# Far edges between the 40th and 41st chunk, biases as rows, index tables worked off later: one change to a graph network and attention kernel

## The reference

```python
aggr = segment_sum(edge_features, receivers_idx, num_segments=num_vertex)
collected = concatenate([layernorm(x), aggr], axis=-1)
h = relu(collected @ W1 + b1)
h = relu(h @ W2 + b2)
x = x + h @ W3 + b3
# then slice attention on layernorm(x): softmax((xn @ W_x + b_x) @ W_slice + b_slice) / temp),
# tokens, attention over 64 slices in 8 heads, and the projection back, added to x
```

## Time and profile before

| | us |
|---|---|
| median of 3 runs | 737.33 |
| the profiled execution's own time | 737.38 |
| its span, first to last instruction | 735.60 |
| first stage: last `first_layer_x` of the stream ends | 286.91 |
| second stage: first `layer1` matmul (L1187) starts | 292.46 |
| PE busy / DVE busy over the span | 711.6 / 408.2 |

### The profile page before, as it was taken

The page is one execution under the profiler, slowest core; times in us unless marked ns, Lnnn a source line. Parts: engine busy times, 40 slices in busy tenths (PEclk is TensorE's granted clock), DMA queues, the critical chain, the costliest instruction groups (busy, mean ns, idle before and its releaser), DMA issues.

```text
span 735.6 us, 12565 instructions
## 1 busy us (share of the span) xinstructions
PE 711.6 (97%) x3716; PEld 456.6 (62%) x3716; DVE 408.2 (55%) x989; ACT 245.5 (33%) x462; POOL 237.3 (32%) x306
## 2 busy tenths in 40 slices
PE   6999999999999997999999989999999999899997
PEld 3666666666666665665666645555555554588886
DVE  6654554554554565244443587878787878522222
ACT  4234333333333344222212133333333333223331
POOL 3101101101110104033233255555656565144441
PEclk8999999999999999999999999999999999999999
DMA  8999999999999995100000000000000000012222
GB/s 318 384 378 415 405 410 410 405 405 407 404 405 406 383 382 173 29 0 0 0 0 0 0 2 0 0 0 0 0 0 0 0 0 1 0 53 76 71 79 70
DMA packets 43233, 118.99 MB, mean 162 GB/s; under 512 B 4937, under 2 KB 19229, under 8 KB 38095
## 3 DMA queue, kind: packets, MB, share of 16 engines
q1 hardware_dynamic: 42399, 118.50, 42.0%
q10 hardware_dynamic: 816, 0.26, 0.2%
HBM read 112.35 MB, written 6.40 MB: 161 GB/s over the span
## 4 chain that ended last, share of the span: by engine, by line
PE 77%; DMA 19%; DVE 2%; issue 1%; SPq 1%; ACT 0%; POOL 0%; DVEq 0%; ACTq 0%; POOLq 0%
DMA ring_mem<-edge_attr_in 18%; PE ps L1089 14%; PE ps L1336 12%; PE ps L1252 11%; PE ps L1260 11%; PE ps L1187 6%; PE ps L1205 6%; PE ps L1195 6%; PE ps L1269 3%; PE ps L1142 3%; PE ps L1244 1%; PE ps L1102 1%; PE ps L1134 1%; DVE big L800 0%; PE ps L1044 0%
## 5 line engine op out<-in xcount | busy, mean ns | idle before, releaser
L1089 PE MATMUL ps<-ring_mem,side 128*64 128x256 f32 x1564 | 188.0, 387 | 7.1 <-DMA ring_mem<-edge_attr_in 5.0
L1089 PEld LDWEIGHTS ps<-ring_mem,side 128*64 128x64 f32 x1564 | 112.6, 138 | 68.2 <-issue 27.5
L717 DVE TENSOR_TENSOR side<-iota_w,rel 128x512 f32<-128x512 f32 x98 | 67.1, 686 | 93.0 <-PE ps L1102 92.8
L1260 PE MATMUL ps<-side,ring_mem 128*128 128x512 f32 x196 | 92.3, 593 | 1.0 <-ACT ring_mem L655 1.0
L1252 PE MATMUL ps<-ring_mem,xn 128*128 128x512 f32 x196 | 92.3, 593 | 0.6 <-DVE ring_mem L952 0.6
L619 ACT ACTIVATE side<-ps 128x256 f32<-128x256 f32 (+1 forms) x98 | 40.6, 414 | 144.4 <-PE ps L1089 142.8
L512 POOL TENSOR_TENSOR var_e<-mv,eps 128x2 f32<-128x2 f32 (+1 forms) x25 | 4.9, 194 | 236.4 <-DVE mv L783 236.4
L800 DVE TENSOR_TENSOR big<-big,ps 128x128 f32 x223 | 63.9, 286 | 30.8 <-issue 12.3
L1336 PE MATMUL ps<-side,ring_mem 128*128 128x256 f32 x360 | 77.9, 379 | 0.0
L566 POOL TENSOR_TENSOR ring_mem<-ring_mem 128x512 f32<-128x512 f32 x49 | 66.9, 1366 | 30.9 <-DVE ring_mem L952 30.9
L1336 PEld LDWEIGHTS ps<-side,ring_mem 128*128 128x128 f32 x360 | 68.4, 190 | 9.3
(11 more groups left out here) (139 smaller groups left out, 883.2 us busy)
## 6 DMA issues: line engine op xcount, KB each, us to landing
ring_mem<-edge_attr_in SPq DMA_DIRECT2D x97, 1024.0 KB, 8.4
x_sb<-x_in SPq DMA_DIRECT2D x24, 256.0 KB, 7.1
result<-ring_mem SPq DMA_DIRECT2D x24, 256.0 KB, 2.1
ring_mem<-edge_attr_in SPq DMA_DIRECT2D x1, 512.0 KB, 6.1
ring_mem<-L_gnn_W_in SPq DMA_DIRECT2D x2, 256.0 KB, 3.5
ring_mem<-L_ffn_W_x_in SPq DMA_DIRECT2D x2, 256.0 KB, 4.6
ring_mem<-L_ffn_W_fx_in SPq DMA_DIRECT2D x1, 512.0 KB, 4.2
ring_mem<-L_ffn_W_out_in SPq DMA_DIRECT2D x1, 512.0 KB, 5.2
```

The lines of the kernel that those rows point to most:

```text
L717: dve.tensor_tensor(hot[:, b], iota_w[:, :].unsqueeze(1).broadcast_to(shape), where.unsqueeze(2).broadcast_to(shape), ALU.is_equal).then_i ...
L1089: last = mm(ps[side_of * WINDOW:(side_of + 1) * WINDOW, SUM_BANKS[s % 2], pair * F:(pair + 1) * F], lhsT=hot[0:parts, s, t, :], rhs=ring8[ ...
L1260: last = mm(ps[:, s % 2, :], lhsT=xn_t[:, s % 2, k, :], rhs=wc[:, k, :], start=(k == 0), stop=(k == KF - 1))
```

## The change

It has six parts. (1) The far block and its branch move on SP, DVE and PE from the end of the stream to between chunk 39 and chunk 40 (`at_whole` in `run_chunks`); all loops are split there. (2) `b1` and `b2` are no longer loaded straight into columns (two loads of 256 single elements), but as four rows of 128, which PE turns after chunk 5 (`bias_columns`) and DVE copies to `b_sb`. These loads and that of `w1a` are now issued by ACT behind its clearing of `agg`, and ACT no longer waits for them before its first copy. (3) DVE's preparation of the tables `two` and `few` moves from before chunk 0 to chunks 2 to 5. (4) `rest_of_table` on PE moves from after chunk 3 to after the sums of chunk 8, and the flag from chunk 5 to chunk 9; the written-out front of PE and DVE is one trip longer (3 in place of 2), that of ACT too (2 in place of 1). (5) SP issues the second chunk ahead of the rest of `dst`, and the first vertex tiles after chunk 2. (6) `fold_transposes` waits only for `W_x` (`wx_in`); the other small loads are waited for by the matmuls that use them.

Before, one loop ran over chunks 8 to 83 and nothing stood there. The diff, with the parts that the steps touch:

```diff
-def run_chunks(eng, step, peel_front, last_trip, total, apart=False):
+def run_chunks(eng, step, peel_front, last_trip, total, apart=False, at_whole=None):
     for t in range(peel_front * UNROLL):
         step(t, t % UNROLL, t // UNROLL, 1 if apart else 2)
-    loops = [(peel_front, WHOLE // UNROLL, 1), (WHOLE // UNROLL, PAIRED // UNROLL, 2)]
-    for lo, hi, groups in loops if apart else [(peel_front, PAIRED // UNROLL, 2)]:
+    for lo, hi, groups in [(peel_front, WHOLE // UNROLL, 1), (WHOLE // UNROLL, PAIRED // UNROLL, 2)]:
         with eng.Fori(lo, hi) as i:
             for s in range(UNROLL):
-                step(i * UNROLL + s, s, i, groups)
+                step(i * UNROLL + s, s, i, groups if apart else 2)
+        if groups == 1 and at_whole:
+            at_whole()
...
+        b_rows = tmp[0:2 * KF, 6144:6272]
...
-                if isinstance(c, int) and c == 0:
+                if isinstance(c, int) and c == 1:
                     rest_of_dst()
                 if isinstance(c, int) and c == 3:
                     sp.wait_ge(x_clear, 1)
                     sp.dma_start(x_sb[0:LAST_ROWS, TILES - 1, :], x[(TILES - 1) * P:N, :]).then_inc(x_tail_in, 16)
-                if s == 0 and before(c, FULL_CHUNKS - 1):
+                if (c == 2 if before(c, UNROLL) and isinstance(c, int) else s == 0) and before(c, FULL_CHUNKS - 1):
                     if past(c, UNROLL):
                         sp.wait_ge(x_in, i * 16)
                     sp.dma_start(tiles_of(i * 2, 2),
                                  x[bass.ds(i * (2 * P), 2 * P), :].rearrange("(t p) f -> p t f", p=P)
                                  ).then_inc(x_in, 16)
-
-            run_chunks(sp, chunk, 1, EDGE_TRIPS, CHUNKS, apart=True)
...
+            def far_chunks():
+                sp.wait_ge(prep_v, 23)
+                far = sp.value_load(far_i[0:1, 0:1], min_val=0, max_val=1)
+                with sp.If(far > 0):
+                    sp.wait_ge(win_psum, WHOLE)
+                    with sp.Fori(0, WHOLE) as c:
+                        reload(c, 1)
+                    with sp.Fori(WHOLE, PAIRED) as c:
+                        reload(c, 2)
+                    with sp.Fori(PAIRED, FULL_CHUNKS) as c:
+                        reload(c, CHUNK_GROUPS)
+                    reload_last()
+                    sp.wait_ge(gen_group, CHUNKS + 1)
+
+            run_chunks(sp, chunk, 1, EDGE_TRIPS, CHUNKS, apart=True, at_whole=far_chunks)
...
+                sp.dma_start(wx[k], w_x[k * P:(k + 1) * P, :]).then_inc(wx_in, 16)
...
-            act.dma_start(w1a_sb[:, :, :], w1[0:F, :].rearrange("(k p) n -> p k n", p=P)).then_inc(mlp_in, 16)
-            act.dma_start(b1_sb[:, :], b1.rearrange("(m p) -> p m", p=P), allow_slow_non_contiguous=True).then_inc(mlp_in, 16)
-            act.dma_start(b2_sb[:, :], b2.rearrange("(m p) -> p m", p=P), allow_slow_non_contiguous=True).then_inc(mlp_in, 16)
             act.wait_ge(agg_clear, 1)
             act.activation(big[:, 0:CLEAR_A], zero[:, 0:1].broadcast_to([P, CLEAR_A]), ACT.Copy).then_inc(agg_clear, 1)
-            act.wait_ge(mlp_in, 16 * 3)
+            for n, b in enumerate((b1, b2)):
+                act.dma_start(b_rows[n * KF:(n + 1) * KF, :], b.rearrange("(m p) -> m p", p=P)).then_inc(b_in, 16)
+            act.dma_start(w1a_sb[:, :, :], w1[0:F, :].rearrange("(k p) n -> p k n", p=P)).then_inc(mlp_in, 16)
...
+            def bases(rows, base, ids):
+                of = ids[0:rows, :].rearrange("c (g e) -> c g e", g=base.shape[1])
+                dve.wait_ge(prep_v, then(dve.tensor_reduce(base, of, AX.X, ALU.min)))
+                dve.wait_ge(prep_v, then(dve.tensor_scalar(base, base, 0.0, float(N), ALU.max, ALU.min)))
...
+                if isinstance(c, int) and c == 2:
+                    dve.wait_ge(dst_in, 16 * 4)
+                    bases(PAIRED - WHOLE, base_two, dst_two)
+                if isinstance(c, int) and c == 3:
+                    relative(PAIRED - WHOLE, base_two, dst_two, rel_two)
+                if isinstance(c, int) and c == UNROLL:
+                    bases(FEW, base_few, dst_few)
                 if isinstance(c, int) and c == UNROLL + 1:
+                    relative(FEW, base_few, dst_few, rel_few)
+                    dve.wait_ge(prep_t, 2)
+                    then(dve.tensor_copy(b_sb[:, :], ps[:, 5, 0:2 * KF]))
+                if isinstance(c, int) and c == 2 * UNROLL + 1:
                     far_flag()
...
+            def far_chunks():
+                with dve.If(far_reg[0] > 0):
+                    dve.wait_ge(groups_added, CREDIT + 2 * WHOLE)
...
             def rest_of_table():
                 pe.wait_ge(prep_v, 15)
+                pe.wait_ge(h1x_ready, 2)
                 base_row(PAIRED - WHOLE, base_two, 5, 128)
                 base_row(FEW, base_few, 5, 256)
                 into_columns(PAIRED - WHOLE, 2, rel_two, 4)
                 into_columns(FEW, CHUNK_GROUPS, rel_few, 5).then_inc(prep_t, 1)
+            def bias_columns():
+                pe.wait_ge(b_in, 16 * 2)
+                tr(ps[:, 5, 0:2 * KF], b_rows, ident[0:2 * KF, 0:2 * KF]).then_inc(prep_t, 1)
+
             def far_row():
+                pe.wait_ge(prep_v, 21)
                 tr(ps[0:1, 5, 0:P], far_one[:, 0:1], ident[:, :]).then_inc(prep_t, 1)
...
                 window_sums(c, s, i, groups)
+                if isinstance(c, int) and c == 2 * UNROLL:
+                    rest_of_table()
                 if s % 2 == 0:
                     return
                 if past(c, UNROLL):
-                    if isinstance(c, int) and c == UNROLL + 1:
+                    if isinstance(c, int) and c == UNROLL + 3:
+                        pe.wait_ge(mlp_in, 16)
+                        pe.wait_ge(prep_v, 16)
+                    if isinstance(c, int) and c == 2 * UNROLL + 1:
                         pe.wait_ge(prep_v, 20)
-                        pe.wait_ge(mlp_in, 16 * 3)
-                    if isinstance(c, int) and c == UNROLL + 3:
-                        pe.wait_ge(prep_v, 21)
+                    if isinstance(c, int) and c == 2 * UNROLL + 3:
+                        pe.wait_ge(prep_v, 23)
+                        far_reg.append(pe.value_load(far_i[0:1, 0:1], min_val=0, max_val=1))
                     if s == 1:
                         ln_transposes(i - 1, 2)
                     else:
                         first_layer_x(i - 1, 2, 1, bank=4)
                 turn(c - 1, s - 1, groups)
                 turn(c, s, groups)
-                if isinstance(c, int) and c == 3:
-                    rest_of_table()
                 if isinstance(c, int) and c == UNROLL + 1:
+                    bias_columns()
+                if isinstance(c, int) and c == 2 * UNROLL + 1:
                     far_row()
-                if isinstance(c, int) and c == UNROLL + 3:
-                    pe.wait_ge(prep_v, 22)
-                    far_reg.append(pe.value_load(far_i[0:1, 0:1], min_val=0, max_val=1))
...
+            def far_chunks():
+                with pe.If(far_reg[0] > 0):
+                    pe.wait_ge(win_ready, WHOLE)
+                    with pe.Fori(0, FULL_CHUNKS) as c:
+                        far_chunk(c, [range(0, UNROLL), range(UNROLL, SUBTILES)])
+                    far_chunk(FULL_CHUNKS, [range(0, UNROLL), range(UNROLL, UNROLL + ROWS_PER_PART)])
+                    pe.wait_ge(gen_group, CHUNKS + 1)
+
+            run_chunks(pe, chunk, 3, EDGE_TRIPS, CHUNKS, at_whole=far_chunks)
+            first_layer_x(EDGE_TRIPS - 1, 2, 0)
+            first_layer_x(EDGE_TRIPS - 1, 2, 1, bank=4)
+
+            def fold_transposes():
+                pe.wait_ge(wx_in, 16 * KF)
+                pe.wait_ge(win_ready, CHUNKS)
+                for k in range(KF):
+                    for j in range(PAIRS):
+                        last = tr(ps[:, k, j * P:(j + 1) * P], wx[k][:, j * P:(j + 1) * P], ident[:, :])
+                last.then_inc(fold_t, 1)
+
+            fold_transposes()
+            pe.wait_ge(groups_added, CREDIT + sums_ahead(CHUNKS - 2, CHUNK_GROUPS))
+            ln_transposes(EDGE_TRIPS, 1, bank=7)
+
             pe.wait_ge(groups_added, CREDIT + ALL_SUMS)
...
             layer2(0, 4 * P, l2_banks)
             pe.wait_ge(h1x_ready, 2 * (EDGE_TRIPS + 1))
+            pe.wait_ge(fold_in, 16 * 5)
             for j in range(PAIRS):
                 for k in range(KF):
```

152 lines of the change are left out of this document (60 added, 92 removed).

## The result

The changed kernel takes 742.92 us (741.68 to 745.01 in 5 runs) against 737.79 us for the kernel before beside it (5 runs): ratio 1.0073, 95% interval 1.0052 to 1.0093, so slower by about 5.4 us. The forecast was 730.6, in a range of 729.4 to 735.0. Forecast and range are wrong, and so is the sign.

The account below looks back on a forecast made before the run. DMA was taken to bound the stream, with PE close behind. From 737.38 us, 5.75 for the stream's end and 1.0 for startup came off, and 0 was added for both moves on PE: 730.6, range 729.4 to 735.0.

Parts of the forecast that it names:

- The end of the stream: Behind the last chunk: no branch or `W_slice` wait starts `layer1` 3.8 us earlier, full clock saves 1.94; together 5.75 us.
- Biases as rows: At startup, 6 to 9 us: without single-element loads DMA's idle time goes and all loads land 1.0 us earlier.
- DVE's preparation: Moved behind chunks 2 to 5: priced at 0, DVE being busy 55% with three one-hots in store.
- Tables between chunks 8 and 9: Tables and flag's row make PE 2.6 us late there; less 1.25 us of spare, 1.35 at chunk 40.
- the spare, 1.25 us in the sum: Chunks 0 to 39: time PE has left over in eight trips, taken to make up lateness.
- The branch at chunk 40: Between chunks 39 and 40: PE 2.68 us late, 4.0 in all, made up before the stream's end.
- Two rivals: At chunk 40: a clock drop, 732.3 us, 20%; a branch waiting behind one chunk's load, 733.1 or 735.0, 22%.
- the rival with one chunk's wait: At chunk 40: the fetch queues behind one chunk's load, stall 5.4 us, total 733.1; 22% with or without clock drop.
- the rival with both: At chunk 40: one chunk's wait plus the clock drop, 735.0 us, within the 22%.
- 8.8 us of loads are in flight: At chunk 40: loads already issued keep DMA full through PE's stall, so PE can catch up.
- the 0.29 us that PE has to spare: Chunks 40 to 83: PE needs 10.71 us of each 10.995 us trip, so 11 trips make up 3.2 us.
- the 1.0 us of room: Last trips: PE's waits of 0.30, 0.36 and 0.34 us, taken to absorb the 0.8 us of lateness left at chunk 84.

Follow-up runs that it names:

- b_tail: Kernel before with `fold_transposes` waiting for `W_x` alone, branch and far block still at the end: 734.10 us, ratio 0.9954.
- b_rows: Kernel before with the biases loaded as four rows and turned by PE behind the tables, `w1a` and biases issued behind ACT's clearing: 737.62 us, ratio 1.0000.
- a_end: Changed kernel with the far block and its branch put back behind the last chunk: 738.14 us, ratio 1.0008.
- x1_dve_early: Changed kernel with far block and branch back at the end and DVE's preparation of both tables back ahead of chunk 0: 736.96 us, ratio 0.9985.
- x2: Changed kernel, far block at the end, PE's branch ahead of `fold_transposes`, tables prepared ahead of chunk 0, tables and biases turned behind chunk 3: 733.23 us, 0.9942.
- a_warm: Changed kernel with five rounds of matmuls with unused results on PE ahead of the branch at chunk 40: 742.16 us, ratio 1.0059.
- b40: Kernel before with only the far block and its branch moved to between chunks 39 and 40 on SP, DVE and PE: 739.66 us, ratio 1.0034.
- a_near: Changed kernel with the far blocks of SP, DVE and PE cut to one operation each, leaving out far edges: 737.80 us, ratio 1.0001.
- d0_split_only: Kernel before with its loops split behind chunk 39 and nothing put there: 737.05 us, ratio 1.0002.
- v1: Kernel before with biases as rows, `fold_transposes` waiting for `W_x` alone, and PE's branch moved ahead of `fold_transposes`: 732.01 us, ratio 0.9929.

## Why the prediction was wrong

**The end of the stream (-5.75).** Right: -5.54 in the trace, 3.87 from the stream's end to the start of `layer1` (1.68 us for 5.55) and 1.67 in `layer1` (3.70 for 5.37), where 3.8 and 1.94 were forecast. Most of it needed no move of the branch: the split of `fold_in` alone gave 3.4 us (b_tail).

**Biases as rows (-1.0).** The size at the start was right (1.2 us at the loads, 0.75 at chunk 8), the conclusion failed: "the stream is bound by DMA from chunk 5 on, so all loads land that much earlier". Alone it is worth 0 (b_rows, 1.0000). The likely reason is that the start only moves the instant from which the loads wait for freed slots, and that PE had no room to free them earlier; no run takes that apart.

**DVE's preparation (0).** Wrong: about 1.7 us (a_end against x1_dve_early, by the ratios). I looked at DVE's share of busy time and at its store of one-hots; the wait came for another thing, the copy of the biases, which stands behind 1.2 us of preparation on DVE and had not been on the list of what is queued behind the moved step.

**Tables between chunks 8 and 9 (2.6 late, less 1.25).** PE's added time was right (0.41 + 2.21). The cost is about 2.6 us (x2): the spare, 1.25 us in the sum, paid for little of it.

**The branch at chunk 40 (2.68, then absorbed).** Two rivals held together. The hole was 4.9 us, near the 5.4 of the rival with one chunk's wait. The clock fell as well, and a_warm prices that at 1.6 us in the traces. But the rival with both was priced at 735.0, and the kernel takes 742.9, because the rivals rested on the same step as the forecast.

**That step is the one that failed:** "8.8 us of loads are in flight, so DMA stays full and PE can catch up by what is spare". With no branch and a full clock, 5.32 us of PE's delay cost 4.2 us in the trace and 4.3 by the ratio, and 2.74 us cost 1.4 and 2.0. Once DMA has been idle, nothing brings that time back: it is the bound afterwards, and the 0.29 us that PE has to spare in each of 11 trips cannot make DMA faster than its 11.0 us a trip. The lateness at chunk 48 (10.1 us) is 10.2 at chunk 83 and still 9.8 at the end of the stream, so of the 1.0 us of room behind chunk 83 only 0.4 was had. I counted PE's spare as room to recover, where it is only room to avoid the loss.

With the measured terms the sum is -5.5 (end) + 1.7 (DVE) + 2.6 (tables) + 6.6 (branch, from b40's stream) = +5.4, against +5.4 measured (1.0073). That they meet so well is partly luck, since the terms come from ratios and from single traces. With the 5.3 us that a_near gained by taking the branch's cost away, the sum is +4.1, and the stream of the change ends 4.8 us behind that of a_end, not 6.6. Where the other 1 to 2 us lie I have not separated; the profiled execution of a_end was itself late at chunk 36 by 5.7 us, the change's by 4.1.

## What to carry over

Where two resources are balanced in a ring, the latency of a queued load is not cover: subtract what an unqueued load needs, and then measure, since here even that was too much; all but about 1 us of a stall on the consumer was lost. A taken branch over a large block costs a code fetch, here about twice as much under a full DMA load; put it where the DMA engines rest, with array work queued ahead of it, and look at what the hole does to the clock. Before a step is moved on an engine, list every small thing queued behind it at its new place, the copies too, not only the large consumers.

## What the runs showed of the hardware

- A taken branch over the far block left PE without work for 4.86 and 4.98 us with the DMA engines full, 1.84 (x1_dve_early) to 2.88 us (d0_split_only) with them nearly idle (25 GB/s at 289 to 291 us in the kernel before), and for nothing visible where the block was one operation long.
- One packet of instruction code (q8) moves at each of these holes, and PE goes on 2.5 to 3.1 us behind it. With the DMA engines full it moved 2.0 us after PE's last matmul, with them nearly idle 0.2 to 0.7 us before that work was done.
- The fetch runs beside array work already issued: 4.46 us of matmuls and 0.75 us of hole instead of 4.86 (a_warm); the packet 1.0 us ahead of the end of the array's work, and 1.57 us of hole ahead of `fold_transposes` instead of 2.03 behind them (v1 against b_tail).
- The granted clock fell from 1.00 to 0.50 (1.2 GHz) within the hole of 4.86 us, in b40 only at the end of its hole of 4.98, and at a hole of 2.03 us (b_tail), but not at 2.43 (a_end) or 1.84 us (x1_dve_early). From the length of a hole alone it can't be told.
- One load of 1 MB landed in 4.8 us with an empty queue; the median in the changed kernel is 8.3, and the one issued last ahead of the stop of the loads took 9.0.
